# Three waits inside GpSimd's row of 32 slot stores

## What is computed

```python
def ffn(x):                                  # x: [1024, 256]
    shared = (silu(x @ sg.T) * (x @ su.T)) @ sd.T * sigmoid(x @ sgate_w.T)   # 704 hidden
    topk_w, topk_ids = top_k(softmax(x @ gate_w.T), 4)                       # 16 experts
    for e in range(16):
        coef = sum(where(topk_ids == e, topk_w, 0), -1)
        acc += (silu_and_mul(x @ w13[e].T) @ w2[e].T) * coef[:, None]        # 176 hidden
    return shared + acc
x = x + 0.5 * ffn(layernorm(x))
x = x + attention(layernorm(x))              # chunked linear attention, rmsnorm, @ Wo.T
x = x + 0.5 * ffn(layernorm(x))
```

## Time and profile before

| | us |
|---|---|
| three runs, median | 546.1 |
| lowest and highest | 544.96, 546.13 |
| profiled execution, own time | 546.05 |
| its span, from first to last instruction | 544.2 |
| TensorE busy | 463.1 (85%) |
| VectorE busy | 239.4 (44%) |
| GpSimd busy | 225.5 (41%) |
| ScalarE busy | 122.2 (22%) |
| GpSimd's 64 slot stores (L710) | 62.8, 982 ns in the mean |

### The profile page before, as it was taken

One profiled execution on the slowest core, in us unless ns is written; L12 is line 12 of the kernel. 1 busy time (PEld: TensorE's weight loads), 2 busy tenths in 40 slices (PEclk: granted clock), 3 DMA queues, 4 the chain that ended last, 5 costly groups with the idle time before them and its releaser, 6 DMA issues.

```text
span 544.2 us, 7022 instructions
## 1 busy us (share of the span) xinstructions
PE 463.1 (85%) x1897; PEld 305.6 (56%) x1898; DVE 239.4 (44%) x708; ACT 122.2 (22%) x352; POOL 225.5 (41%) x188
## 2 busy tenths in 40 slices
PE   6949639899999999955968889990989999999992
PEld 4625315566666666632548874640566666666651
DVE  6551012254444454465394648300234444454436
ACT  3200000122222222123545542100112222222210
POOL 0057720055556555600034302775015666556540
PEclk9979777999999999985988988996799999999996
DMA  8999871178887666550000000323006666666647
GB/s 265 339 396 388 213 273 65 37 163 151 154 156 115 105 103 106 73 153 13 0 1 0 2 2 21 115 107 120 2 21 101 104 118 103 102 104 109 109 52 230
DMA packets 49591, 65.18 MB, mean 120 GB/s; under 512 B 5435, under 2 KB 45243, under 8 KB 48955
## 3 DMA queue, kind: packets, MB, share of 16 engines
q1 hardware_dynamic: 32947, 43.36, 26.2%
q0 software_dynamic: 16608, 21.37, 24.7%
HBM read 30.94 MB, written 33.77 MB: 119 GB/s over the span
## 4 chain that ended last, share of the span: by engine, by line
PE 63%; another core or an unknown queue 9%; DMA 9%; DVE 8%; SPq 5%; issue 5%; ACT 1%; POOL 0%; DVEq 0%; POOLq 0%
PE ps L380 19%; PE ps L398 13%; PE ps L355 6%; PE ps L332 5%; PE ps L387 5%; DMA sums<-ar,idx 4%; PE ps L337 4%; SPq L254 3%; PE ps L366 3%; PE ps L452 3%; DMA WS<-wsh 2%; DMA back<-sums 2%; PE ps L515 2%; DVE X L917 1%
## 5 line engine op out<-in xcount | busy, mean ns | idle before, releaser
L721 POOL DMA_INDIRECT sums<-ar,idx x94 | 145.4, 1547 | 163.8 <-DVE ar L898 109.9
L380 PE MATMUL ps<-W,ar 128*128 x376 | 131.4, 472 | 1.2 <-issue 1.2
L398 PE MATMUL ps<-W,ar 88*128 x376 | 97.0, 380 | 1.4 <-DVE ar L891 1.4
L710 POOL DMA_INDIRECT slots<-XR,pos x64 | 62.8, 982 | 69.5 <-DMA slots<-zeros 30.6
L355 PE MATMUL ps<-WS,ar 128*128 128x256 f32 (+1 forms) x192 | 52.8, 426 | 37.3 <-DVE ar L799 15.3
L885 DVE SCALAR_TENSOR_TENSOR ar<-ps,xs,ar 128x176 f32<-128x176 f32 x94 | 37.7, 401 | 104.2 <-issue 62.5
L380 PEld LDWEIGHTS ps<-W,ar 128*128 128x128 f32 x376 | 63.7, 189 | 25.4 <-issue 1.9
L594 ACT ACTIVATE ar<-ps 128x176 f32<-128x176 f32 x94 | 29.8, 317 | 188.6 <-PE ps L380 186.7
L355 PEld LDWEIGHTS ps<-WS,ar 128*128 128x128 f32 (+1 forms) x192 | 40.1, 213 | 55.0 <-issue 39.0
L398 PEld LDWEIGHTS ps<-W,ar 88*128 88x128 f32 x376 | 64.0, 190 | 7.4 <-issue 1.9
L332 PE MATMUL ps<-XT,WS 128*128 128x512 f32 x96 | 54.1, 692 | 0.0
(11 more groups left out here) (130 smaller groups left out, 383.3 us busy)
## 6 DMA issues: line engine op xcount, KB each, us to landing
xs<-slots SPq DMA_DIRECT2D x94, 138.0 KB
slots<-zeros SPq DMA_DIRECT2D x1, 6486.0 KB, 26.1
W<-w SPq DMA_DIRECT2D x4, 1408.0 KB
back<-sums SPq DMA_DIRECT2D x16, 256.0 KB, 3.0
W<-w SPq DMA_DIRECT2D x1, 2816.0 KB
sums<-zeros SPq DMA_DIRECT2D x2, 1152.0 KB
sums<-zeros SPq DMA_DIRECT2D x18, 128.0 KB
sums<-ar,idx POOLq DMA_INDIRECT x94
```

What stands on the lines that cost most here:

```text
L380: mm = pe.matmul(ps[:, 4 + i % 2, 0:2 * FE], xt[i % 2][:, k * P:(k + 1) * P], w, start=k == 0, stop=k == KD - 1)
L398: mm = pe.matmul(ps[:, 2 + i % 2, 0:D], ht[i % 2][:, c * P:(c + 1) * P], w, start=c == 0, stop=c == 1)
L710: pool.indirect_dma_start(out=slots_dram[:, :], out_offset=bass.IndirectOffsetOnAxis(ap=pos[:, t, r:r + 1], axis=0), in_=XR[:, t, :], in_o ...
L721: pool.indirect_dma_start(out=sums_dram[f][a][:, :], out_offset=bass.IndirectOffsetOnAxis(ap=idx[:, i:i + 1], axis=0), in_=ys[i % NY], in_ ...
```

## The change

In `dispatch`, behind the last store of token tiles 1, 3 and 5 (the 8th, 16th and 24th store of the row), GpSimd waits until `s_disp` has counted all stores issued so far, in this pass and the ones before. Then it goes on.

```diff
@@ -710,6 +710,9 @@
                         pool.indirect_dma_start(
                             out=slots_dram[:, :], out_offset=bass.IndirectOffsetOnAxis(ap=pos[:, t, r:r + 1], axis=0),
                             in_=XR[:, t, :], in_offset=None).then_inc(s_disp, 16)
+                    if t in (1, 3, 5):
+
+                        pool.wait_ge(s_disp, 16 * TOPK * (NT * f + t + 1))
```

## The result

The changed kernel takes **532.4 us** in the median of 4 runs (531.77 to 533.23), the kernel before 546.07 (544.96 to 546.13). The ratio is 0.9755, with a 95% interval from 0.9737 to 0.9774. The profiled execution took 532.48 us with a span of 530.6 us, against 546.05 and 544.2. The forecast was 528.5 us.

A forecast was written before the change was run, and what follows sets the result against it. TensorE's semaphores, late beside GpSimd's unbroken row of store issues, were taken to bound both FFN passes. Gains of 7.4 us in pass 0 and 10.2 in pass 1 took 546.05 to 528.5 us; range 518 to 553.

The forecast's parts named there:

- What bounds the kernel: Shared expert's units: GpSimd's unbroken store issues make TensorE's semaphores late, with waits of 21.05 and 19.76 us.
- Why the breaks suffice: Store row: each batch of 8 takes 10.2 us, under the 15.8 us still on time, so the stall is gone.
- Price of a wait in pass 1: GpSimd's row: 2.2 us per wait, 1.9 us beyond usual idle; three move the last landing from 378.4 to 384.1.
- Pass 0, the second batch: Stores 9 to 16 beside weight loads: land at 65, bounds 61 and 68; slot loads at 90.3, pass gain 7.4 us.
- a clock: Start of the expert tiles: TensorE's lower clock after idling, charged at 2.5 us in each pass.
- Pass 1: Second FFN pass: stores set the first expert tile's start, 386.4 + 2.5 instead of 399.07, a gain of 10.2 us.
- The gap from slot loads to the first tile: Ahead of the expert tiles: the first slot load takes 2.3 us, in both passes.
- Rival A: Store row: waits cost and clear nothing, stores under way cause the lateness; slower, 568 us, chance 0.22.
- The rule of the Trainium skill: DMA waits: issue early, do other work, wait late on the semaphore; by it the change can only lose.
- Rival B: Store row: pauses only delay the filling, about 0.27 us per store; half the gain, 537 us, chance 0.17.

The follow-up runs named there:

- e2: Changed kernel with four semaphores, one per eight stores; the 17th and 25th store wait only for the batch before the last: 530.83 us, ratio 0.9754.
- e3: Changed kernel with its landing waits replaced by two scratch fills that GpSimd waits for, behind the 8th, 16th and 24th store: 522.21 us, ratio 0.9579.
- e4: Changed kernel with two landing waits instead of three, behind the 12th and 24th store: 533.61 us, ratio 0.9782.
- e9: Changed kernel with the load of `W2` split into four, packets of 8192 bytes, on the 513.31 us chip: 527.66 us, ratio 1.0305.
- e10: e8 with the load of `W2` split into four, on the 513.31 us chip: 512.95 us, ratio 1.0007.
- e11: Store row left unbroken, six scratch fills of 128x1000 behind the 32nd store, on the 513.31 us chip: 513.33 us, ratio 1.0005 to the kernel before.
- e12: The changed kernel run again, unchanged, where the kernel before takes 545.87 us: 533.58 us, ratio 0.9789.
- e13: e8 run again, unchanged, where the kernel before takes 545.87 us: 519.4 us, ratio 0.952.
- e5: e3 with one scratch fill of 128x1000 at each break, 1.2 us between stores: 518.06 us, ratio 0.9486.
- e6: e3 with tiny scratch fills behind every second store instead: 531.85 us, ratio 0.9767.
- e8: e3 with scratch fills of 128x1000 and 128x400 at each break, 1.7 us between stores: 518.74 us, ratio 0.9511.
- e1: Changed kernel with the three landing waits in pass 1 alone: 534.41 us, ratio 0.9796.

## Why the prediction was right, and where it was off

**What bounds the kernel: right.** TensorE's late semaphores were behind both stalls, and breaking GpSimd's row removed them, as no "remote" release of L583 is left in after. e2 and e3 separate the pause in the issue from the landing: e2 limits what is under way and, without a pause, keeps the stall; e3 pauses without a landing and loses it. What it is that fills up stays unnamed, as it was.

**Why the breaks suffice: the reason was wrong, the outcome right.** The step was "Every batch is 8 stores, 10.2 us, well under the 15.8 us at which semaphores were still on time. The stall is then gone". It takes each break to start the count anew. e4's batches of 12 stores, 15.2 us of issue, are under 15.8 us too, and semaphores became late in pass 1. A break leaves a rest; with eight stores and 1.8 us the rests stay small enough. That the forecast held here is in part luck.

**Price of a wait in pass 1: right, slightly high.** 1.9 us was forecast above the usual 0.3; measured are gaps of 1.82, 1.83 and 1.93, so 1.5 to 1.6 above it. The row of pass 1 grew by 4.75 us (47.01 from first store to slot loads, 42.26 before) instead of 5.7.

**Pass 0, the second batch: wrong.** The step "At most they need the 17.6 us plus 1: 68" failed. Its first part was near: the last packet of the first batch was through by 50.4 instead of 48.6. That of the second was through by 72.95, 5 us outside the bound, and SyncE's loads came at 96.84 instead of 90.3. I had counted packets in total: 766 packets by 66.2 are 16 stores' worth, but by then GpSimd was at its 27th store, so they need not be those of the first 16. A store has landed only with its last packet, and with no more than 8 stores issued at a time GpSimd waits for just that one. That it was held up among the 32768-byte packets of `W2` is what e4's last 37 packets, e9's split and the pair e10 and e11 speak for. The pass gave 1.5 us instead of 7.4: 6.5 for the late loads, less 0.6 for a clock that cost 1.9 instead of 2.5.

**Pass 1: 12.1 us instead of 10.2**, 0.95 from the row and 0.9 from the clock (1.6 instead of 2.5). Together 13.6 instead of 17.6 us: 5.9 too much in pass 0, 1.9 too little in pass 1, so the errors cancel in part. It gives 546.05 − 13.6 = 532.5, the profiled execution's time.

**The gap from slot loads to the first tile: right.** 2.3 us was taken, 2.25 and 2.23 were measured.

**Rival A fell** on the chips with the lateness: no stall returns behind the pauses. On the chip without it, e9 had rival A's sign for a reason it did not give: there was nothing to clear. The rule of the Trainium skill named beside it ("DMA: Bandwidth & Descriptors", "Rules for kernel authors") fits in one half. Waiting early for the landings cost 14.2 us against a pause of like effect (e12, e13). What won was the break, not the wait.

**Rival B** was right as a mechanism (e4, e5, e6), and its own counting fits the runs; what did not follow from it was its outcome. By that counting (an estimate) eight stores add 2.2 us, a pause takes off its own length, and the limit is 3.8 us. A shorter pause leaves a rest, but the rest does not have to reach the limit: three of 0.3 to 0.4 us plus 2.2 make 3.2 in the changed kernel, and three of at most 0.5 make 3.7 at most in e8, just short. In e5, with pauses of 1.2 us, the third batch passes it (2 × 1.0 + 2.2 = 4.2), which is where its lateness began, and in e4 it is reached 8 to 9 stores into the second batch. So batches of eight come to the limit only with pauses below about 1.7 us ((4 × 2.2 − 3.8) / 3). The counting is coarse: for e6 it gives the 17th or 18th store, and pass 1 showed the 19th to 21st.

**What the prediction could not see** is the chip. The kernel before took 546.07 us in the first pair and 545 to 546 on three of the four chips of the experiments, and 513.3 on the fourth, which was used in one session only.

## What to carry to other kernels

When a semaphore arrives long after the work that raises it, look at what another engine issues at that time, and test it with a pause there that waits for nothing: e8's form is worth 4.9% on the chips with the lateness and, with the `W2` split (e10), costs nothing on the one without. A wait for DMAs to land is a poor pause, since its price goes up with whatever large packets are under way beside the stores (12.73 us in pass 0 against 1.83 in pass 1). A gain of this kind should be timed on more than one chip: with landing waits it was −2.4% in the first pair and, as e9 (with `W2` split), +3.1% on another chip.

## What the runs showed that was not expected

- An unbroken row of indirect stores came with TensorE's semaphores late by up to 20 us in the kernel before, in e1's pass 0 and in e2's pass 1, and with none late in e11 on another chip. The same kernel before took 545 to 546 against 513.3 us.
- The traces of the two kinds differ in one more thing. The 64 stores raise `s_disp` 1024 times. On the chip without lateness (e9, e10, e11) the trace records all 1024; elsewhere it records 292 (before), 621 (after), 405 (e4), 483 (e8) or 596 (e12). So records of semaphore updates are missing in the runs on the chips where the kernel before takes 545 to 546 us, also in those where no semaphore is late. Whether both come from one cause, and whether recording has a part in the lateness, no run shows.
- The lateness follows the issue, not the transfers: it ended 3.5 us behind a stop in the middle of a row (e2, pass 0), 4.2 us behind the end of one (e2, pass 1), 4.7 and 3.8 us in the kernel before.
- A gap of 1.7 us between stores behind every eighth is enough, 1.2 us holds to about the 24th store, 0.1 us per pair to the 19th to 21st (pass 1).
- A load of 88 packets of 32768 bytes took 21.6 us (e4), at 2.20 us per packet and most of the time 9 to 11 at once. GpSimd's wait for stores issued beside such a load was 12.73 us (after) and 14.01 us (e12), where pass 1 has 1.82 to 1.93.
